# Two transformer layers on one core: the second layer's output projection moved into the attention's block

## The reference

```
x = x + L1_attn(layernorm(x))      # 16 heads, causal softmax, then the output projection
    o_ckv = einsum('bhqk,bkr->bqhr', softmax(scores), ckv)        # r = 64 per head
    y     = einsum('bqhr,hre->bqe', o_ckv, w_o_abs)               # w_o_abs: 16 heads x 64 -> 256
x = x + L1_ffn(layernorm(x))
    hidden = silu(x @ W1.T) * (x @ W3.T)                          # 256 -> 1024, twice
    out    = fwht(hidden) @ W2.T                                  # Walsh-Hadamard transform of 1024, then 1024 -> 256
```

## Time and profile before

| | |
|---|---|
| median of 3 runs | 2289.82 us (2288.16 to 2292.33) |
| profiled execution, own time | 2300.19 us |
| its span, first to last instruction | 2298.7 us |
| PE busy / DVE busy / ACT busy | 1993.8 (87%) / 1451.2 (63%) / 1256.6 (55%) |
| mean granted TensorE clock | 0.928 of full |

### The profile page before, as it was taken

How to read it: one execution, slowest core, us unless ns; L and a number is a source line. 1 busy time by engine, 2 the same in 40 slices (tenths; PEclk the granted TensorE clock), 3 DMA queues, 4 the chain that set the end, 5 groups by cost and what they waited for, 6 DMA issues and landing times. The chain is left out here.

```text
span 2298.7 us, 41540 instructions
## 1 busy us (share of the span) xinstructions
PE 1993.8 (87%) x11702; PEld 1336.9 (58%) x11766; DVE 1451.2 (63%) x3115; ACT 1256.6 (55%) x2558; POOL 882.9 (38%) x899
## 2 busy tenths in 40 slices
PE   4987999999767679999648899999698999996698
PEld 1552333333345469999624577777545777775587
DVE  4887888888355579999257566665265555543443
ACT  0793777777533147777114577777144777771322
POOL 1340000000054647797053277777001666670100
PEclk7896999999967889999869899999898999998899
DMA  7953000000531259898321012112000111012000
GB/s 210 289 104 56 2 0 0 1 0 1 126 118 59 83 168 267 263 287 266 106 69 41 10 45 53 42 42 56 14 0 1 24 24 35 21 35 68 1 19 19
DMA packets 185938, 173.83 MB, mean 76 GB/s; under 512 B 19651, under 2 KB 170741, under 8 KB 184822
## 3 DMA queue, kind: packets, MB, share of 16 engines
q1 hardware_dynamic: 173750, 143.23, 22.6%
q0 software_dynamic: 10720, 29.44, 3.9%
q10 hardware_dynamic: 1376, 0.02, 0.0%
HBM read 96.15 MB, written 61.60 MB: 69 GB/s over the span
## 5 line engine op out<-in xcount | busy, mean ns | idle before, releaser
L2638 POOL TENSOR_TENSOR w_rest<-work,w_head 128x512 fp32r<-128x512 f32 (+3 forms) x384 | 395.4, 1041 | 224.9 <-ACT w_head L2595 222.6
L790 DVE TENSOR_REDUCE half_max<-m_ps 128x1 f32<-128x512 f32 x512 | 317.2, 683 | 58.2 <-PE m_ps L712 57.6
L2484 DVE TENSOR_REDUCE piece_max<-m_ps 128x1 f32<-128x512 f32 (+3 forms) x384 | 201.1, 549 | 205.9 <-PE m_ps L2411 161.7
L847 ACT ACTIVATE weights<-s_ps 128x512 f32<-128x512 f32 x512 | 266.2, 601 | 108.2 <-PE s_ps L730 108.2
L2591 ACT ACTIVATE work<-s_ps 128x512 f32<-128x512 f32 (+3 forms) x384 | 187.4, 488 | 103.0 <-PE s_ps L2439 79.0
L2595 ACT ACTIVATE w_head<-work 128x512 fp32r<-128x512 f32 (+3 forms) x384 | 201.3, 524 | 56.9 <-PE o_ps L2448 46.7
L712 PE MATMUL m_ps<-kT,qT 96*128 (+1 forms) x512 | 204.3, 400 | 8.5 <-DVE half_max L790 6.6
L730 PE MATMUL s_ps<-qT,kT 99*128 (+1 forms) x512 | 193.3, 384 | 9.5 <-DMA qT<-max_rows 5.1
L2448 PE MATMUL o_ps<-w_head,lat_head 128*128 128x512 f32 (+3 forms) x384 | 184.4, 480 | 1.4 <-POOL w_rest L2638 1.4
L887 POOL COPY v_now<-v 128x83 f32 (+1 forms) x64 | 16.0, 256 | 366.6 <-PE o_ps L742 361.7
L1095 POOL TENSOR_TENSOR gv_rest<-ex_wgv,gv_head 128x736 fp32r<-128x736 f32 x64 | 113.9, 1779 | 75.8 <-ACT gv_head L1192 75.8
(11 more groups left out here) (395 smaller groups left out, 5050.8 us busy)
## 6 DMA issues: line engine op xcount, KB each, us to landing
slots<-zero SPq DMA_DIRECT2D x8, 3456.0 KB, 27.5
rows<-slots SPq DMA_DIRECT2D x64, 256.0 KB, 3.4
slots<-ex_out SPq DMA_DIRECT2D x64, 256.0 KB, 3.0
ex_wgv<-in_L_ffn_wg_dram SPq DMA_DIRECT2D x72, 176.0 KB, 3.0
ex_wgv<-in_L_ffn_wv_dram SPq DMA_DIRECT2D x72, 176.0 KB, 3.3
ex_wo<-in_L_ffn_wo_dram SPq DMA_DIRECT2D x72, 128.0 KB, 3.2
oT<-work SPq DMA_DIRECT2D x64, 128.0 KB
w_down<-l_inverse SPq DMA_DIRECT2D x32, 256.0 KB
```

The costliest lines, as they stand in the source:

```text
L790: dve.tensor_reduce(half_max[:, u:u + 1], m_ps[:, BANK[u], :], AX.X, ALU.max).then_inc(max_done, 1)
L847: act.activation(w[:, s % 2 * 4 + j, :], s_ps[:, BANK[4 * s + j], :], ACT.Exp, scale=HD ** -0.5).then_inc(w_done, 1)
L2484: dve.tensor_reduce(piece_max[:, qt, k0 // 512:k0 // 512 + 1], m_ps[:, r % 2, 0:n], AX.X, ALU.max).then_inc(d["max_done"], 1)
L2638: pool.tensor_tensor(w_rest[:, s % 3, c0:512], w[:, s % 3, c0:512], w_head[:, s % 3, c0:512], ALU.subtract).then_inc(d["w_rest_done"], 1)
```

## The change

The projection moves into `l1_attend`'s block, behind the last head, for both batches. It uses five of the attention's PSUM banks instead of two new ones: the two of `m_ps` and the three of `s_ps`. TensorE waits until pair 6 is scaled (`scaled` at 7 of 8) and the banks have been read, takes 7 products for each of the tiles 0 to 4, waits for pair 7, adds the eighth product to each of the five, and then does tiles 5 to 7 whole. Batch 1's statistics (`ln3b`) move into batch 0's block with it, and the two `bn_stats` per tile into batch 1's. In the last block only `ffn_weights` and the final statistics are left. W1 and W3 get a semaphore of their own and are loaded on SyncE's queue at the start of batch 1's `l1_attend`, into the memory of `w_q`, which `l1_project` has then finished with; `w_q` is declared with 128 partitions for this, where it had 96 (the same bytes per partition). TensorE transposes W1 and W3 before W2 instead of after it. W2 and the Hadamard table are still loaded at the start of the last block, which is now behind the whole projection.

```diff
-def l1_output(block, d, b, oT, w_o, x, y_ps, tiles=range(TB), taken=None):
-    n0 = TB * b
+            if taken is None:
+                @block.vector
+                def _(dve):
+                    dve.wait_ge(d["added"], T * TOPK)
+
+                layernorm_stats_in(block, l, m, "ln3b", x, mean_var, rstd, t0=TB, t1=T)
+            banks = [m_ps[:, 0], m_ps[:, 1], s_ps[:, 0], s_ps[:, 1], s_ps[:, 2]]
+            y = [banks[t % len(banks)][:, 0:D] for t in range(TB)]
+            l1_output(block, d, b, oT, w_o, x, y, ((h0 + H1) * NR + FREE_M, (h0 + H1) * NC + FREE_S), taken)
+
+def l1_output(block, d, b, oT, w_o, x, y, free, taken=None):
+    OPEN = 5
+    n0, p0 = TB * b, HP * b
     @block.tensor
     def _(pe):
-        for t in tiles:
-            reuse(pe, d["y_added"], t + n0, 2)
+        def product(t, p):
+            return pe.matmul(y[t], oT[:, p, t * P:(t + 1) * P], w_o[:, p, :], start=p == 0, stop=p == HP - 1)
+
+        pe.wait_ge(d["scaled"], p0 + HP - 1)
+        pe.wait_ge(d["max_done"], free[0])
+        for t in range(OPEN):
+            if t == 2:
+                pe.wait_ge(d["w_done"], free[1])
+            for p in range(HP - 1):
+                product(t, p)
+        pe.wait_ge(d["scaled"], p0 + HP)
+        for t in range(OPEN):
+            product(t, HP - 1).then_inc(d["y_done"], 1)
+        for t in range(OPEN, TB):
+            pe.wait_ge(d["y_added"], t + n0 - OPEN + 1)
             for p in range(HP):
-                i = pe.matmul(y_ps[:, t % 2, 0:D], oT[:, p, t * P:(t + 1) * P], w_o[:, p, :], start=p == 0,
-                              stop=p == HP - 1)
+                i = product(t, p)
             i.then_inc(d["y_done"], 1)
...
@@ def l1_attend, SyncE
+                if preload is not None:
+                    preload(sp)
                 pair_of(0, True)
@@ def ffn_weights
-        raw = l.sb("w13_raw", [P, 2, FK, D])
-            for i, n in enumerate(("W1", "W3")):
-                sp.dma_start(raw[:, i, :, :], a[f"L1_ffn_{n}"].rearrange("(f p) n -> p f n", p=P)
-                             ).then_inc(d["loaded"], 16)
             sp.dma_start(raw2[:, :, :], a["L1_ffn_W2"].rearrange("(k p) n -> p k n", p=P)).then_inc(d["loaded"], 16)
             sp.dma_start(had[:, :], a["hadamard_table"]).then_inc(d["loaded"], 16)
...
-            pe.wait_ge(d["loaded"], 64)
+            pe.wait_ge(up_loaded, 32)
...
+            pe.wait_ge(d["loaded"], 32)
...
@@ def transformer
+            def load_up(sp):
+                for i, n in enumerate(("W1", "W3")):
+                    sp.dma_start(raw[:, i, :, :], a[f"L1_ffn_{n}"].rearrange("(f p) n -> p f n", p=P)
+                                 ).then_inc(up_loaded, 16)
...
-            with ExitStack() as ctx3, nc.psum_tensor("y1_ps_1", [P, 2, 512], F32) as y_ps, nc.Block() as block:
-                l1_output(block, d, B - 1, oT, l1_weight[2], x, y_ps, range(2), taken)
-                ffn_weights(block, nc, next_layer, c, a, w_up, w_down)
-                l1_output(block, d, B - 1, oT, l1_weight[2], x, y_ps, range(2, TB), taken)
+            with ExitStack() as ctx3, nc.Block() as block:
+                ffn_weights(block, nc, next_layer, c, a, raw, up_loaded, w_up, w_down)
                 layernorm_stats_in(block, Mem(nc, ctx3), next_layer, "ln4", x, mean_var, rstd, taken=taken)
```

More of the change, by code:

```diff
@@ L2332, in l1_attend @@
     if later is not None:
-        x, slot, weight, slots, got = later
+        slot, weight, slots, got = later
     with ExitStack() as ctx:
@@ L2678, in _ @@
     def _(dve):
-        for t in tiles:
+        for t in range(TB):
             dve.wait_ge(d["y_done"], t + n0 + 1)
-            dve.tensor_tensor(x[:, t + n0, :], x[:, t + n0, :], y_ps[:, t % 2, 0:D], ALU.add
-                              ).then_inc(d["y_added"], 1)
+            dve.tensor_tensor(x[:, t + n0, :], x[:, t + n0, :], y[t], ALU.add).then_inc(d["y_added"], 1)
             if taken is not None:
@@ L2723, in layer1_attention @@
             l1_attend(nc, m, c, d, b, qT, kT, lat_head, lat_rest, oT, w, parted, staged, scale, sums_dram,
-                      shiftT, (x, slot, weight, slots, spare) if b == 0 else None)
-            if b < B - 1:
-                with ExitStack() as ctx2, nc.psum_tensor("y1_ps_0", [P, 2, 512], F32) as y_ps, nc.Block() as block:
-                    layernorm_stats_in(block, Mem(nc, ctx2), m, "ln3b", x, mean_var, rstd, t0=TB, t1=T)
-                    l1_output(block, d, b, oT, w_o, x, y_ps)
+                      shiftT, x, w_o, mean_var, rstd, (slot, weight, slots, spare) if b == 0 else None,
+                      taken if b == B - 1 else None, preload if b == B - 1 else None)
     return d
@@ L2735, with ffn_weights @@
 FK = F1 // P
[L2738 removed]
+def ffn_weights(block, nc, m, c, a, raw, up_loaded, w_up, w_down):
     with ExitStack() as ctx:
         l = Mem(nc, ctx)
[L2744 removed]
         raw2 = l.sb("w2_raw", [P, DK, F1])
@@ L2762, in _ @@
         def _(pe):
-            pe.wait_ge(d["loaded"], 64)
+            pe.wait_ge(up_loaded, 32)
             n = 0
-            for f in range(FK):
-                reuse(pe, d["copied"], n, 4)
-                for k in range(DK):
-                    i = pe.transpose(turn_ps[:, n % 4, k * P:(k + 1) * P], raw2[:, k, f * P:(f + 1) * P],
-                                     c.ident[:, :])
-                i.then_inc(d["turned"], 1)
-                n += 1
             for w in range(2):
@@ L2779, in _ @@
                     n += 1
+            pe.wait_ge(d["loaded"], 32)
             for f in range(FK):
-                pe.wait_ge(d["copied"], f + 1)
+                reuse(pe, d["copied"], n, 4)
+                for k in range(DK):
+                    i = pe.transpose(turn_ps[:, n % 4, k * P:(k + 1) * P], raw2[:, k, f * P:(f + 1) * P],
+                                     c.ident[:, :])
+                i.then_inc(d["turned"], 1)
+                n += 1
+            for f in range(FK):
+                pe.wait_ge(d["copied"], 2 * FK + f + 1)
                 reuse(pe, d["had_copied"], f, 2)
@@ L2788, in _ @@
             n = 0
-            for f in range(FK):
-                act.wait_ge(d["turned"], n + 1)
-                act.activation(w2T[:, f, :], turn_ps[:, n % 4, 0:D], ACT.Copy).then_inc(d["copied"], 1)
-                n += 1
             for w in range(2):
@@ L2799, in _ @@
                     n += 1
+            for f in range(FK):
+                act.wait_ge(d["turned"], n + 1)
+                act.activation(w2T[:, f, :], turn_ps[:, n % 4, 0:D], ACT.Copy).then_inc(d["copied"], 1)
+                n += 1
         @block.vector
```

20 lines of the change are left out of this document (11 added, 9 removed).

## The result

| | before | after |
|---|---|---|
| median (runs) | 2291.07 us (4) | 2265.64 us (4) |
| lowest to highest | 2288.16 to 2298.21 | 2261.99 to 2266.36 |
| span of the profiled execution | 2298.7 us | 2264.1 us |
| last output of batch 0 | 1614.57 | 1601.29 |
| from there to batch 1's first xh | 42.97 | 28.46 |

The ratio is 0.9882, 95% interval 0.986 to 0.9903, which is 22 to 32 us off 2291. The spans of the two profiled executions differ by more, 34.6 us. The table takes them apart at points that both kernels have (the last output is put 0.04 us ahead of VectorE's copy of it, as the modelled ends of matmuls and these copies stand throughout). 13.3 us of the difference arise ahead of the first handover, where the instructions are the same; the handovers give 14.5 and 11.2 us; 1.3 and 3.0 us are lost behind them.

What follows compares the result with a forecast made beforehand. TensorE bounds the attention, but idles over 12 us at each of two handovers to the projection. Gains of 14.5 and 10.0 us sum to 24.5, from the median 2289.8 to 2265.3 us; range 2259 to 2276, forecast chance 0.80.

Steps and rivals of the forecast that it cites:

- First handover: Batch 0's attention to projection: 35 products fill TensorE's wait for pair 7, 64 run without pause; gain 14.5 us (12.5 to 14.8).
- the wait ahead of tile 5: First handover's projection: tile 5 waits for tile 1's add, with a margin of 0.2 us; if missed, some tenths.
- the 1.95 us of the cold start: First handover before the change: 64 products took 29.57 us instead of 27.6 at full clock.
- Second handover: Batch 1's last output to the statistics' end: projection fills the gap, W2's load becomes visible; gain 10.0 us (4.7 to 11.8).
- I take 6.4 us, between the two: Last block: load time of W2 and the Hadamard table, 3.0 us of bytes plus a fixed part between 2.6 and 4.2.
- a landing of 5.6 to 7.2 us: Sign that the forecast is right: the duration that W2's DMA row should show in the changed kernel.
- Rival 2: Last block: W2 lands late because its 3.09 us issue is its own; gain 4.7 instead of 10.0, 2270.6 us; chance 0.06.
- Rival 1: Weights block runs at the low clock between projection and Hadamard products: 5.8 us more, 2271.1 us; chance 0.10.
- Rival 3: Both handovers: first product still held until pair 7 is scaled, gap unfilled; 2294.2 us, or 2300.0 if cold; chance 0.02.
- Rival 4: Attention: the handovers' gain is given back by 0.8 us per head over 32 heads, time moves little; chance 0.02.
- The sum: Whole kernel: 14.5 + 10.0 = 24.5 us off the median 2289.8, giving 2265.3 us.
- starts cold in both cases: Feed-forward part's start: TensorE idle 15.98 us before, some 22 after, cold either way; costed at nothing.

Runs made afterwards that it cites:

- held kernel: The changed kernel with TensorE's first projection product waiting until all eight pairs are scaled (8 instead of 7): median 2293.89 us, against 2292.84 for the kernel before.
- products while idle: The changed kernel plus 18 float32 products nobody reads, on TensorE in the block that splits the weights: median 2265.57 us.

## Why the prediction was right, point by point

**First handover: right, 14.5 us.** Forecast from the last output to xh 28.4 us, measured 28.46 or 28.47 in every kernel that has it whole. The products took 0.4316 us each, pair 7 came before the 35 open ones were done, and the wait ahead of tile 5 cost nothing: the statistics ended at 1617.36 and tile 5 was due 40 products after 1601.13, at 1618.4. That wait was misread by one tile: its value is 1 for tile 5, so it asks for tile 0's add, which ended at 1617.7, and not for tile 1's. The margin was so 0.7 us and not 0.2, and nothing else in the sum hangs on it. Even the warm clock was in the sum, as the 1.95 us of the cold start; where TensorE still waits in full, it cost 1.9 to 2.8 us in the first handover and 2.1 in the held kernel's second.

**Second handover: right in its mechanism, its gain forecast 1.2 to 1.6 us too small.** Forecast 52.6 us, measured 51.43, 51.05, 51.04. The term that was mis-sized is the landing of W2 and the table, "I take 6.4 us, between the two": from W2's issue to the first of its transposes it was 5.45 us (2073.38 to 2078.83) in the first profile, 5.08 and 5.06 in the other two, which is all that sets the three apart. What ended last was the table, issued 0.43 us behind W2 and landed 4.97 us later, 0.5 us after W2. Of the two fixed parts that bounded the term, 2.6 and 4.2 us, the small one was nearer, as 5.45 and 5.06 less 3.0 us of bytes are 2.4 and 2.1. The larger came from a queue with 3 MB ahead. The signs "a landing of 5.6 to 7.2 us" and a wait of "1 to 3 us" so came out short, with at most 5.4 us to the table's landing and waits of 1.05, 0.66 and 0.65 us. The Trainium skill's fit (DMA: Bandwidth & Descriptors, "Anatomy of one DMA") is for DMAs that GpSimd issues; the estimate from it for both loads, 4.6 us, is 0.4 to 0.8 us short of what SyncE's loads took here and nearer than the 6.4. The transposes of W1 and W3 took 4.36 instead of 4.59 us, which is off the path, as TensorE waits behind them. The rest, 16.9 us from W2's transposes to the end, was forecast as 17.1.

**Rival 2, W2 lands late.** It did not come: the 3.09 us of W2's issue were not its own. Alone it took 0.39 us; behind W1 and W3 it took 3.09 and 3.12 in the kernel before, 2.34 with the first handover only and 1.21 with W1 and W3 loaded late. The argument that "the two larger issues ahead" took 1.03 us together was wrong in one thing, as W1, W3 and W2 are of one size, 1 MB each.

**Rival 1, a cold weights block.** It did not come in any of the kernels that fill the gap, but it was no idle thought: it happened in one of the two executions of the kernel before. Its price was too high, though: W2's 16 records took 3.68 us cold, where the rival had 4.6 (the 8 records in 2.30 us that it was read from still took 1.74 us in the kernel with products while idle, at a clock of 1.00, so the clock was not all that held them). The sum had taken the first profile of before as typical in this; against the second the second handover's gain is 12.8 us. With W1 and W3 late, TensorE did nothing but transposes after 10.25 us of idle time: the first 32 took 6.44 us, the next 16 took 2.28 us, and the clock rose from 0.50 to 1.00 while only transposes ran. The Trainium skill (TensorE: Matmul & The Clock Gate, Part 4, PE-mode transpose) says of transposes, with figures for bf16, that they do not count as busy and do not bring the full clock; these float32 transposes did.

**Rival 3, held for pair 7.** It was tried as written. In the profile it has 43.29 and 65.49 us, where the working had 42.7 and 67.3. The forecast of 2294.2 us was met (2293.89) partly by luck, as it stood on 2289.8 for the kernel before, which had 2292.84 on this chip: 4.4 us more were forecast, the medians give 1.0 and the ratio 0.7 less to 9.4 more. That the order of the rest costs without the gap is seen in the profile (2.9 or 1.2 us in the second handover); the times do not show it.

**Rival 4, the gain given back in the attention.** From batch 1's first xh to its last output the changed kernel took 413.89 to 415.41 us, 0.7 to 2.3 more than the one before, and not the 13 us in one batch that the rival needs.

**The sum.** 24.5 us were forecast, and the handovers give 25.7 (14.5 + 11.2) to 27.6 us by the profiles, depending on which of before's two stands for it; with the 61.59 us of the first handover only as a third it could be 24.7. The chips' comparisons give 25.4, 32.9 and 20.7 us, around it. That the median was met within 0.4 us is partly luck: the gain was 0.9 us larger than forecast and the kernel before's median 1.3 us higher, which offset each other, and the chip of the third comparison has the changed kernel at 2275.5 us. "I take the gain from the median" was the right choice: the profiled execution's 10.4 us above it seem to lie ahead of the handovers, as its last output of batch 0 came 8.9 us later than the mean of the fourteen profiles, and 2275.7 us, the sum against its own time, would have been 10 us off.

**What was costed at nothing.** The feed-forward part "starts cold in both cases": it does, but how long it stays so varies, 152.87 to 155.92 us, in the kernel before (152.87, 155.20) as in the changed one (155.92, 152.94, 153.02). The 3.0 us that the first pair of profiles shows lost there are not the change's. The early load of W1 and W3 was costed at nothing too: both had landed 8.9 us after the first was issued (1739.73), and the queue's next issue came at 1753.81. Of the 1.3 us between the handovers nothing was forecast; it remains unexplained and is of the size of its own spread.

## What to carry to other kernels

Where an engine waits at a stage's end for one last piece of a sum, do the sums' other terms in that wait, and open as many accumulators as the wait can be filled with: here 2 banks filled half of it and gave a third of the gain, because the clock still fell in the half that stayed idle (3.2 us in the first handover). Look then at what the filled work used to cover: a load and a chain of another engine became visible behind it, and without the filled gap the same order gained nothing. And compare two profiles stretch by stretch at points that both have, since the part of this kernel that the change does not touch varies by more than the change's own terms are uncertain.

## What the runs showed of the hardware

- Five accumulations left open in five PSUM banks while others proceed cost nothing that can be seen: the 64 products took 0.4316 us each, the pace of the kernel before.
- Transposes alone brought the full clock back, from 0.50 to 1.00, after 10.25 us of idle time (W1 and W3 loaded late).
- After its work ended, TensorE kept the full clock through pauses of 1.44 and 1.05 us in the weights block (clock 1.00). In the pause of 6.05 us with two tiles open it was at 1.00 for the first 4.9 us and had fallen when work came back. After 3.31 us it was cold in one execution of the kernel before, after 3.47 us warm in another, and after 2.90 us warm with the first handover only.
- Once work came back, the moment at which the clock rose varied between executions of the same kernel. The changed kernel, first and second execution, TensorE's timeline from the feed-forward part's first transposes to the products at full pace:

```profile
2108.65 2.29 PE L2888 MATMUL x_ps<-ident,xh 128*128 128x128 f32 x8 [22.94 <-DVE xh L2968]
...
2118.07 0.62 PE L154 MATMUL g_ps<-x_rest,up_head 128*128 128x512 f32 x1
...
2118.76 0.40 PE L154 MATMUL g_ps<-x_head,up_head 128*128 128x512 f32 x1
```

```profile
2111.42 2.30 PE L2888 MATMUL x_ps<-ident,xh 128*128 128x128 f32 x8 [22.93 <-DVE xh L2968]
...
2117.43 0.63 PE L154 MATMUL g_ps<-x_head,up_rest 128*128 128x512 f32 x1
...
2118.26 0.40 PE L154 MATMUL u_ps<-x_rest,up_head 128*128 128x512 f32 x1
```

The transposes start at 2108.65 and 2111.42, and the 0.63 us products become 0.39 us ones at 2118.5 in the first and at 2118.1 in the second, 9.8 and 6.7 us later.

- Filling the idle stretch ahead did not keep the clock: at 1.00 in 2104 to 2108, it was 0.74 and 0.69 behind the first, sparse work (products while idle).
